# A GRU scan by segments ahead of a mixture of experts: the input product of r and z added on TensorE, steps written out, fp16 state in the rough steps

## The reference

```python
def cell(h, x):
    gi = x @ W_ih + b_ih
    gh = h @ W_hh + b_hh
    i_r, i_z, i_n = jnp.split(gi, 3, axis=-1)
    h_r, h_z, h_n = jnp.split(gh, 3, axis=-1)
    r = jax.nn.sigmoid(i_r + h_r)
    z = jax.nn.sigmoid(i_z + h_z)
    n = jnp.tanh(i_n + r * h_n)
    h_new = (1.0 - z) * n + z * h
    return (h_new, h_new)
...
    logits = flat_x @ Wg + bg
    top_vals, top_idx = jax.lax.top_k(logits, TOPK)
...
        h = jax.nn.gelu(tok @ W1[i], approximate=False)
        y = h @ W2[i] * p
        out = out.at[sel_idx].add(y)
```

## Time and profile before

| | |
|---|---|
| median of 3 runs | 984.72 us (983.96 to 1125.22) |
| profiled execution | 983.88 us |
| its span, first to last instruction | 982.1 us |
| PE busy in the span | 801.9 us (82%), 11202 matmuls |
| PEld busy | 513.3 us (52%) |
| DVE busy | 682.0 us (69%), 2339 instructions |
| ACT busy | 421.9 us (43%), 844 instructions |
| POOL busy | 200.8 us (20%) |
| chain that ended last | PE 55%, DVE 26%, issue 9%, ACT 4% |

### The profile page before, as it was taken

One profiled execution on the slowest core, in us unless ns is written; L12 is line 12 of the kernel. 1 busy time (PEld: TensorE's weight loads), 2 busy tenths in 40 slices (PEclk: granted clock), 3 DMA queues, 4 the chain that ended last, 5 costly groups with the idle time before them and its releaser, 6 DMA issues.

```text
span 982.1 us, 29964 instructions
## 1 busy us (share of the span) xinstructions
PE 801.9 (82%) x11202; PEld 513.3 (52%) x11203; DVE 682.0 (69%) x2339; ACT 421.9 (43%) x844; POOL 200.8 (20%) x507
## 2 busy tenths in 40 slices
PE   5968798898777677777776614599999999999996
PEld 2434444477667676677776603344444444444442
DVE  5968677767888788888888566666666767665600
ACT  1636455554444344444444240273447407334700
POOL 1002111133333333333333000101201110120011
PEclk9989999999999999999999755599999999999999
DMA  9700000000000000000000437123615352361012
GB/s 344 255 1 2 2 2 2 2 3 2 0 0 0 1 2 0 0 0 0 0 0 0 173 85 259 44 89 127 193 21 187 112 126 87 128 192 22 1 13 30
DMA packets 20100, 61.61 MB, mean 63 GB/s; under 512 B 2064, under 2 KB 2064, under 8 KB 17424
## 3 DMA queue, kind: packets, MB, share of 16 engines
q1 hardware_dynamic: 15744, 52.46, 15.1%
q0 software_dynamic: 3584, 8.42, 4.8%
q10 hardware_dynamic: 720, 0.03, 0.0%
HBM read 52.49 MB, written 12.62 MB: 66 GB/s over the span
## 4 chain that ended last, share of the span: by engine, by line
PE 55%; DVE 26%; issue 9%; ACT 4%; POOL 2%; DVEq 2%; DMA 1%; POOLq 0%; SPq 0%; ACTq 0%
PE ps L482 17%; PE ps L495 17%; PE ps L340 11%; PE ps L332 5%; DVE wa L925 5%; DVE halves L946 4%; DVE wa L935 3%; DVE wa L930 3%; DVE ocand L939 2%; ACT wa L578 2%; PE ps L424 2%; PE ps L315 2%; POOL halves L720 2%; DVE hx L951 1%; PE ps L470 1%
## 5 line engine op out<-in xcount | busy, mean ns | idle before, releaser
L340 PE MATMUL ps<-halves,wa 128*128 128x64 f16 x8448 | 295.0, 194 | 94.5 <-DVE halves L946 76.7
L340 PEld LDWEIGHTS ps<-halves,wa 128*128 128x128 f16 x8448 | 271.1, 99 | 140.1 <-DVE halves L946 93.7
L578 ACT ACTIVATE wa<-wa,un_gates 128x128 f32<-128x128 f32 x288 | 111.8, 396 | 185.4 <-DVE wa L925 180.8
L482 PE MATMUL ps<-wb,big 128*128 128x512 f16 x768 | 168.8, 382 | 1.5 <-DVE wb L1231 1.5
L495 PE MATMUL ps<-big 128*128 128x512 f16 x768 | 166.9, 379 | 0.0
L925 DVE TENSOR_TENSOR wa<-ps,big 128x128 f32<-128x128 f32 x288 | 80.3, 285 | 75.7 <-PE ps L340 73.7
L583 ACT ACTIVATE wa<-wa,un_gates 128x64 f32<-128x64 f32 x288 | 99.0, 344 | 73.9 <-DVE wa L935 73.9
L482 PEld LDWEIGHTS ps<-wb,big 128*128 128x128 f16 x768 | 75.2, 98 | 93.0 <-issue 4.4
L495 PEld LDWEIGHTS ps<-big 128*128 128x128 f16 x768 | 75.2, 98 | 89.9
L332 PE MATMUL ps<-hx,wb 128*128 128x512 f16 x432 | 110.3, 388 | 8.6 <-DVE hx L870 8.6
L641 ACT ACTIVATE hx<-ps,un_hid_in 128x512 f32<-128x512 f32 x64 | 43.8, 684 | 114.1 <-PE ps L482 114.1
(11 more groups left out here) (166 smaller groups left out, 624.4 us busy)
## 6 DMA issues: line engine op xcount, KB each, us to landing
wa<-in_w SPq DMA_DIRECT2D x32, 1024.0 KB, 5.6
hs_rows<-big SPq DMA_DIRECT2D x8, 516.0 KB, 6.1
big<-in_w_ih SPq DMA_DIRECT2D x3, 1024.0 KB, 11.5
hx<-in_x_t SPq DMA_DIRECT2D x3, 1024.0 KB, 19.8
big<-in_w_hh SPq DMA_DIRECT2D x4, 768.0 KB, 16.3
wa<-in_x_t SPq DMA_DIRECT2D x1, 1024.0 KB, 5.0
hx<-hs_rows,idx POOLq DMA_INDIRECT x16
out<-hx,idx_out POOLq DMA_INDIRECT x16, 4.9
```

The lines of the kernel that those rows point to most:

```text
L340: mm = pe.matmul(gate_ps[:, j, g, :], whh_parts[:, k, w, (4 * g + j) * P:(4 * g + j + 1) * P], halves[:, src, k, h, :], start=(k == 0 and ...
L482: mm = pe.matmul(ps[:, m % 2, :], w1p[:, w, k, m * P:(m + 1) * P], tokT[:, t, k, :], start=(k == 0 and n == 0), stop=(k == KD - 1 and n == 2))
L578: act.activation(rz[:, j, :, :], pre[:, j, :, :], ACT.Sigmoid, scale=un_gates[:, 0:1]).then_inc(S["sig_done"], 1)
```

## The change

**Input product of r and z.** `gi` for r and z is kept as two fp16 halves (`gi_rz`), written by ScalarE (HIGH, `tile` and `first_tile`) and VectorE (LOW, `rz_low`) straight from the fill's bank. At the beginning of each j of a step TensorE multiplies it by a scaled identity (`diag`, bf16) into the gates' PSUM (`inject`), with `start=True`; all other matmuls of a step accumulate. Rough steps inject the high half only, one matmul of 128 columns for each j. Exact steps inject both halves: in steps 20 to 23 two of 128 columns for each j, from step 24 on four of 64, since the update gate z has its own banks there (`update_ps`, banks 4 to 7, `apart`). `pre_rz` is gone.

**Sigmoids.** ScalarE takes r and z apart, 64 columns each, out of PSUM, with the bias as a per-partition operand. Where r and z share a bank, z waits until VectorE has read the bank (`rn_done`).

**Rough steps** have the state as fp16 high half only: `keep_state` is left out of them and GpSimd multiplies z by the half. The low halves of W_hh are made in steps 4 to 15 (`whh_low`), 512 columns at a time, and no longer before step 0.

**Segment shifts.** The last step before a shift writes its blend into columns 1 to 15 of each sequence's segments and the first column from the initial state (`moved`, `first_column`). The copies of `shift` remain only after `check`.

**Steps written out.** Steps 24 to 71 are straight code on all engines. `ORDER`, `FILLS` and the orders on VectorE and ScalarE are new.

```diff
-        FILLS = (9, 3, 3, 3)
+        FILLS = (13, 2, 2, 1)
...
+            def inject(j, c, cols, parts, steps, apart):
+
+                pe.wait_ge(S["rn_done"], steps + j + 1)
+                pe.wait_ge(S["z_done"], steps + j + 1)
+                scaled = diag[:, 1 if c in (1, 2) else 0, :]
+                for part in parts:
+                    if apart:
+                        for g in range(2):
+                            pe.matmul(gate_of(j, g, True), scaled, gi_rz[:, c, j, part, g, cols],
+                                      start=(part == HIGH), stop=False, skip_group_check=True)
+                    else:
+                        pe.matmul(gate_ps[:, j, 0:2, :], scaled, gi_rz[:, c, j, part, :, cols],
+                                  start=(part == HIGH), stop=False, skip_group_check=True)
...
-            for i in range(ROUGH, FILLED):
-                fill(FILL_STEP * i, FILL_STEP * i + FILL_STEP)
-                gates(i % 2, made(i), lows(i), KD * i)
...
+            for i in range(ROUGH, FIRST + L):
+                if i < FILLED:
+                    fill(FILL_STEP * i, FILL_STEP * i + FILL_STEP)
...
+                gates(i % 2, *place(i), made(i), lows(i), KD * i, i >= FILLED)
...
-                def sig(j):
-                    act.wait_ge(S["pre_ready"], base + j + 1)
-                    act.activation(rz[:, j, :, :], pre[:, j, :, :], ACT.Sigmoid,
-                                   scale=un_gates[:, 0:1]).then_inc(S["sig_done"], 1)
+                def reset_gate(j):
+                    act.wait_ge(S["gates_mm"], base + j + 1)
+                    act.activation(rz[:, j, 0, :], gate_ps[:, j, 0, :], ACT.Sigmoid, bias=bsum[:, j:j + 1],
+                                   scale=un_gates[:, 0:1]).then_inc(S["r_done"], 1)
+
+                def update_gate(j):
+                    if apart:
+                        act.wait_ge(S["gates_mm"], base + j + 1)
+                    else:
+                        act.wait_ge(S["rn_done"], base + (KD + j + 1))
...
+                alone = ((reset_gate, 0), (update_gate, 0), (reset_gate, 1), (update_gate, 1), (tanh, 0),
+                         (reset_gate, 2), (tanh, 1), (update_gate, 2), (reset_gate, 3), (tanh, 2),
+                         (update_gate, 3), (tanh, 3))
+                shared = ((reset_gate, 0), (reset_gate, 1), (update_gate, 0), (tanh, 0), (reset_gate, 2),
+                          (update_gate, 1), (tanh, 1), (reset_gate, 3), (update_gate, 2), (tanh, 2),
+                          (update_gate, 3), (tanh, 3))
...
-                for f, j in ((pre_rz, 0), (pre_rz, 1), (reset, 0), (candidate_in, 0), (reset, 1), (pre_rz, 2),
-                             (candidate_in, 1), (one_less_z, 0), (pre_rz, 3), (reset, 2), (blend, 0), (candidate_in, 2),
-                             (one_less_z, 1), (reset, 3), (blend, 1), (one_less_z, 2), (candidate_in, 3), (keep_state, 0),
-                             (blend, 2), (keep_state, 1), (one_less_z, 3), (keep_state, 2), (blend, 3), (keep_state, 3)):
+                exact = ((reset, 0), (candidate_in, 0), (reset, 1), (candidate_in, 1), (one_less_z, 0), (blend, 0),
+                         (reset, 2), (one_less_z, 1), (candidate_in, 2), (blend, 1), (reset, 3), (candidate_in, 3),
+                         (keep_state, 0), (keep_state, 1), (one_less_z, 2), (one_less_z, 3), (blend, 2), (keep_state, 2),
+                         (blend, 3), (keep_state, 3))
+                rough = ((reset, 0), (candidate_in, 0), (reset, 1), (candidate_in, 1), (one_less_z, 0), (reset, 2),
+                         (blend, 0), (candidate_in, 2), (one_less_z, 1), (reset, 3), (blend, 1), (candidate_in, 3),
+                         (one_less_z, 2), (blend, 2), (one_less_z, 3), (blend, 3), (other_work, 0))
```

374 lines of the change are left out of this document (222 added, 152 removed).

## The result

The changed kernel is slower. It takes 1022.02 us (median of 4 runs, 1021.71 to 1023.81) where the kernel before took 983.96 and 984.72 us in its two undisturbed executions (its other two, of 1001.9 and 1125.22 us, are left out): a ratio of 1.0387, 95% interval 1.0362 to 1.0412. The forecast was 935.4 us, so it missed by 86.6 us. The profiled execution took 1021.78 us.

The account below looks back on a forecast made before the run. A ring over three engines bounds each step. From 983.88 us: start -4.3, rough -9.2, filled +1.5, burn-in -9.8, second shift -4.7, real run -21.6, last step -0.4, together -48.5: 935.4 us; range 921 to 949, widened to 914 to 958.

Parts of the forecast that it names:

- The change, rough steps: Part of the prediction on the rough steps, 19 intervals: 6.2 us a step, bounds 5.5 and 6.6, saving 9.2 us.
- Twelve fills end at 2.6: Rough step on TensorE: front fills end at 2.6 us, then it stands 0.8 us until the last injection at 3.4.
- three rivals: Whole kernel: TensorE becomes the bound (901 us, 0.11), ring keeps its length (956, 0.18), or slower through instruction supply (0.03).
- The one that ended slower: Written-out steps: straight code cannot be supplied with instructions; at 7.1 us a step 1003 us; rival's chance 0.03.
- The side work: Rough steps on VectorE: low halves and x_low, at most 3.0 us a step; 0.25 added in each of four steps.
- The lower bound of 5.5: Rough step: 5.5 us if TensorE never waits for a gate, counting fills, four blocks and injections.
- The +1.5: Filled exact steps (36.84 us): injections show in full, +1.85, and the last interval gets 0.4 shorter, together +1.5.
- Two more sums leave VectorE ... -0.40: Exact step, reset product to last low half: two sums fewer at 0.2 us a VectorE slot, -0.40.
- +0.1: Exact step on ScalarE: twelve instructions for eight make the first tanh start at about 1.2 instead of 1.02, +0.1 us.
- The dependent pairs: Exact step on VectorE: new order puts three dependent pairs side by side, starts 0.32 or 0.33 behind, not 0.2: +0.36 us.
- The reset product's +0.44: Head of the exact step: reset product starts 0.44 us behind the one sigmoid out of PSUM, saving 0.32.
- The second rival: Exact steps: ring keeps its length, 6.1 us, through same-engine waits and ScalarE's twelve instructions; 956 us, chance 0.18.

Follow-up runs that it names:

- e1: The changed kernel with each r or z low half made in the step in which ScalarE makes its high half: 957.38 us, ratio 0.972.
- e2: The kernel before with steps 24 to 71 written out as straight code, in its own orders: 967.3 us, ratio 0.9821.
- e8: e7 with ScalarE's order of the rough steps also used in the exact steps: 947.31 us, ratio 0.9603.
- e9: e7 with ScalarE's rough order changed, reset gates of j=2 and j=3 ahead of the tanhs of j=0 and j=1: 952.5 us, ratio 0.9664.
- e10: e9 with fifteen fills at the front instead of thirteen and the injections behind the fourteenth: 944.84 us, ratio 0.9592.
- e14: e7 with fifteen front fills, injections behind the fourteenth, and ScalarE's and VectorE's rough orders changed for an earlier last update gate: 933.34 us, ratio 0.9467.
- e15: e7 with fifteen front fills, injections behind the fourteenth, and filled exact steps' tiles and low halves made ahead of each step's own work: 931.3 us, ratio 0.9447.
- e7: e1 with VectorE's exact order of the kernel before, less its four sums, instead of the new order: 944.59 us, ratio 0.9575.
- e12: e7 with GpSimd's instructions in the steps narrowed to one column, all waits kept, state not the reference's: 928.77 us, exact step 5.43 us.
- e3: The changed kernel without any low halves of the r and z input product, exact steps injecting the high half only: 951.05 us, ratio 0.9655.

## Why the prediction was wrong, point by point

**The step that failed.** In "The change, rough steps" `rz_low` was costed as work of VectorE ("its slots are taken by rz_low, x_low and whh_low of 0.75 each") and the fills as free to run ("Twelve fills end at 2.6"). The order rows of TensorE ahead of the prediction show a fill with `[waits gi_low]`, and the prediction never asks when that low half is made. Of the waits for banks it prices only those at the injections. The rough stage is 49.5 us over its forecast and the filled one 21.5; e1, which moves the release alone, takes back 47.9 and 16.4 of them. In the filled stage VectorE's low half comes at 235.10 behind its last work of the step, and TensorE waits 3.27 us.

```profile
234.96 0.23 DVE L1081 TENSOR_TENSOR halves<-carried,halves 128x64 f16<-128x64 f32 x1
235.10 0.68 DVE L959 SCALAR_TENSOR_TENSOR big<-ps,big 128x512 f16<-128x512 f32 x1
...
235.84 2.74 PE L360 MATMUL ps<-hx,wb 128*128 128x512 f16 x6 [3.27 <-DVE big L959]
```

None of the three rivals held this mechanism. The one that ended slower was about instruction supply, and it did not happen: 89 packets for 32, and no idle time of TensorE above 0.15 us without a wait in the written-out steps. The chance of 0.02 for slower stood for that one named way to lose, and nothing stood for the waits that had not been looked at. By the Trainium skill (Runtime: NRT & Kernel Launch, Instruction fetch mechanics) straight code is read ahead; e2's written-out steps of 5.93 for 6.30 agree, while e8's nine stretches of 0.20 to 0.66 us without a shown wait are not explained by it.

**Rough steps, once the release is mended.** Forecast 6.2, e1 6.18. The last injection starts 3.43 us behind the first fill (92.80 to 96.23), forecast 3.4, and 0.84 behind the first injection, forecast 0.8; the profile calls only 0.31 of it idle, since three injections run meanwhile. The stage is 120.4 for 118.8. More than these 1.6 lies at steps 8 and 16, whose intervals are 7.69 and 7.37: TensorE waits there for ScalarE's last tile of the chunk, a wait that the text does not price.

```profile
109.67 0.56 PE L389 MATMUL ps<-big,diag 128*128 128x128 f16 x4 [1.77 <-ACT big L615]
```

The side work cost less than allowed, 0.17 in each of two steps and not 0.25 in four. That the last injection waits for the last update gate is confirmed by e9, e10 and e14. The lower bound of 5.5 for a step in which TensorE does not wait was reached by e14 (5.51).

**Filled exact steps.** The +1.5 was right for what it counted: e15 has 38.32. e1's 43.4 contains the wait for the last low half ahead of step 24, the same kind of wait, which the text did not name either.

**Exact steps.** 5.65 was forecast, 6.00 measured, worth 5.6 + 11.4 us. The base was right: 5.28 and 0.65 behind it make 5.93, which is e2's step. The terms that were wrong are "Two more sums leave VectorE ... -0.40" and ScalarE's "+0.1" beside it, -0.30 together. With and without the sums the stretch is 4.59 and 4.68 us (e2, e7): +0.09. The prediction let VectorE's slots set the length of the whole stretch and looked at ScalarE's queue only up to the first tanh. In e7 that queue holds the reset products up to the last one, 2.25 us behind the first, so what the sums gave back was taken. Behind it VectorE sets the pace, and there GpSimd's instructions cost it 0.27 (e12). What a shorter ScalarE queue would give stays open. The dependent pairs were priced at 0.36 and cost 0.28 (e1 against e7). The reset product's +0.44, the new state at 2.3 and the covered injections (e3) were right. The second rival, a ring that keeps its length (6.1), described the exact steps better than the forecast did. Part of its mechanism, ScalarE's twelve instructions in the sums' place, is what e7's rows show; e8 put them in another order and did not make them fewer.

**Shifts, start, end.** The second shift took 6.07 us, forecast 6.35. The first fill started at 55.98, 5.6 us sooner than before (61.55), forecast 4.3, and the first reset product stands at 62.0, 6.2 ahead of the first gate sum of before (68.16). From the start of the last step to the end the kernel takes 447.0 us for 446.8, forecast 446.4. In the order of time, -1.9 (start), +49.5 (rough), +21.5 (filled), +5.6 (burn-in), -0.3 (shift), +11.4 (real run) and +0.6 (end) make 86.4, the miss of the profiled execution (1021.78).

**The clock.** Behind some of TensorE's long waits the trace shows half rate, and with the waits gone the two stages have a granted clock of 1.00 (e15) for 0.93 and 0.89. Six fills take 1.47 us behind the wait that ends at 80.42 and 2.74 behind the one that ends at 235.84. There the wait costs more than its own length. It is not so behind each: from 75 to 129.6 us TensorE waits 3.50 and 1.31 in turn, and the granted clock is 1.00.

## What to carry to other kernels

When an instruction is moved to an engine that reads a buffer, price the buffer's release before the instruction's length: ask who fills that buffer next, when in the reading engine's order the read stands, and whether it runs beside the writer. A queue that does "the last step's leftovers" after its own work is a bad place for a read that frees a bank; here 0.68 us of work cost up to 3.5 us a step, and the cure was to issue it one step sooner. Taking instructions off an engine shortens a ring only if that engine's slots set its length: look which other queue has grown, and compare the same stretch with and without them before counting slots. And in a ring, work moved from behind a wait to ahead of it pays in full until the engine is dense (0.216 per fill here).
